# The first adjacency tiles are turned in quarters between the last rows, the loads of Y and of the sums are gated by turned rows, and the last pair's outputs are made by halves

## The chip, the cores and the metric

The kernel runs on one core of a Trainium2 chip. The metric is the device time of one execution in microseconds, the median of several runs; lower is better.

## The reference, cut to what matters

```python
scores = einsum('nd,md->nm', x @ Wq.T + bq, key @ Wk.T + bk) / sqrt(N)
s = scores * adj
s = where(abs(s) < 1e-05, -1e9, s)
u = softmax(s) @ (value @ Wv.T + bv)
x1 = layernorm(x + u @ Wm.T + bm)
out = layernorm(x1 + relu((adj @ x1) @ W1.T + b1))
```

x is 4096 x 512 in float32, adj is 4096 x 4096 of zeros and ones, every weight is 512 x 512.

## The kernel before, in words

A tile is 128 rows, so there are NT = 32 tiles of rows and columns. A float32 matrix enters TensorE as a high and a low float16 part, and a product of two such takes three passes.

The attention runs in 64 steps, g = 0 to 63: 32 tiles against the first half of the keys, then the same 32 against the second half (g = 32 + n). In a step of the second half TensorE makes the scores of tile n, the product of row tile n - 4 with W1 (`rows_product`, L895), the weighing of the values with the probabilities of tile n - 1 (`weigh`, L860) and the projection of the merged row n - 2 (`project`, L881). Between them VectorE and ScalarE mask, exponentiate, merge the two halves, normalise to x1 and split it. Every operand of TensorE that lies the wrong way round is turned by a DMA transpose which SP issues: PT from the probabilities Phl (`turn_prob`, L373 and L376), UT from the merged row Uhl (`turn_merged`, L483 and L486), x1T from the split row x1hl (`turn_x1`, L470 and L473), and AT from the adjacency matrix in bfloat16, adj_bf (`adj_tile`, L491: one tile of 128 rows by 4096 columns, 1 MB). There is one x1T and it is overwritten: the turn of row n waits until `rows_product(n - 1)` is done (y_mm).

The products of x1 with W1, called Y, go to DRAM as they come (`store_y`, L477). GpSimd loads them back in chunks of four tiles, 1 MB each (`load_y`, L698), into Y, which stays in SBUF for the last stage; chunk c has tiles 4c to 4c + 3, and the last four tiles (28 to 31) are written to Y directly. Signed sums of Y's quarters go to DRAM too, and come back as Ta and Tb (`load_sums`, L704). The places of Y, AT, Ta and Tb lie over the keys, values and probabilities, which is what some waits in SP's and GpSimd's code are for.

The last stage multiplies the adjacency matrix with Y. The rows are taken in pairs p of tiles p and 16 + p. Pairs 0 and 1 are made plainly (`aggregate(p, k, m0, m1)`, L955: matmuls for column tiles m0 to m1 of one row tile, two each), the other 14 by a scheme of seven products in place of eight (`seven`, `product`, L986), with sums of adjacency blocks (`adj_sum`, L1901) and of Y. Pair q = p - 2 has its outputs put together on VectorE (`pair`): sums of products into `csum` (L1908), sums of those (L1913), then `output` (L1856 scale and bias, L1860 relu and the row x1, L1863 statistics) and `result` (mean, nine steps of an inverse root, L1872). The four plain outputs go through the same `output` and `result`, and count on f_out. The sums of the last tiles of Y are made in between by `joined` (L1825), `last_sums` and `signed_low` (L1836).

The order of work is written out by hand, engine by engine. Each engine runs its own list in order, and waits on semaphores; SP's list is also the order in which its DMAs are issued, and all its transposes pass through it. So the tail of the attention reads on TensorE:

```python
weigh(2 * NT - 1, 1, NT - 1)
rows_product(NT - 4)
project(2 * NT - 2, 0, NT - 1)
aggregate(0, 0, 0, NP // 2)
aggregate(0, 0, NP, NP + 8)
rows_product(NT - 3)
project(2 * NT - 1, 1, NT - 1)
```

## Time and profile before

| | |
|---|---|
| median of 3 runs | 2114.94 us (2113.25 to 2116.5) |
| the profiled execution | 2114.64 us |
| its span in the trace | 2113.0 us |
| TensorE busy | 2045.3 us, 97% |
| VectorE busy | 1464.9 us, 69% |
| ScalarE busy | 675.2 us, 32% |
| granted TensorE clock, mean | 0.988 |

The times in the trace are counted from the span's start. The attention ends at about 1674 us, and the seven-product pairs begin at 1761 us. On SP and GpSimd a row of the order of time gives how long the engine was held by issuing a DMA, not how long the data took; "to landing" is the time from issue to arrival. A number in square brackets on a row is the time for which the engine stood idle before it, with what ended that.

### The profile page before, as it was taken

To read this page: it belongs to the slowest core of one execution; us is meant where nothing else is said; L and a number is where in the kernel's file an instruction comes from. 1 tells how busy PE (TensorE), PEld (TensorE's weight loads), DVE (VectorE), ACT (ScalarE), POOL (GpSimd) and SP (SyncE) were. 2 spreads that over 40 slices of the span, in tenths; PEclk is the share of its full clock that TensorE was granted. 3 is DMA by queue.
4 is the path that set the end of the run, shared out by engine and by line. 5 is a ranking of instruction groups with operands and counts; after the bars stand their busy time and mean duration, and the time that the engine had idled before them with its cause. 6 is when DMAs were issued, how large, how long until landed. Compare 5 with 4: busy or idle time off the path is not lost.

```text
span 2113.0 us, 29747 instructions
## 1 busy us (share of the span) xinstructions
PE 2045.3 (97%) x9471; PEld 980.5 (46%) x9471; DVE 1464.9 (69%) x3348; ACT 675.2 (32%) x884; POOL 81.2 (4%) x139
## 2 busy tenths in 40 slices
PE   7987999999999999999999999999999899999997
PEld 6873444444444444444444444444444334444443
DVE  3876656656565656687777777778878557877887
ACT  3343434344443434343333333333343210000000
POOL 1110000000000000000000000000000000000000
PEclk9998999999999999999999999999999999999999
DMA  7676876676667676887666666677777985554551
GB/s 244 223 271 152 189 182 151 171 162 168 160 165 176 147 172 155 216 183 161 159 163 163 163 163 163 166 170 183 186 181 211 223 239 127 131 121 119 138 133 56
DMA packets 586289, 359.56 MB, mean 170 GB/s; under 512 B 500992, under 2 KB 505088, under 8 KB 585856
## 3 DMA queue, kind: packets, MB, share of 16 engines
q1 hardware_dynamic: 564672, 275.07, 52.0%
q0 software_dynamic: 21568, 83.89, 16.4%
q8 instruction: 24, 0.39, 0.1%
q14 instruction: 25, 0.20, 0.0%
HBM read 181.15 MB, written 88.60 MB: 128 GB/s over the span
## 4 chain that ended last, share of the span: by engine, by line
PE 88%; DVE 5%; SPq 3%; DMA 3%; ACT 1%; issue 1%; DVEq 0%; ACTq 0%
PE ps L840 31%; PE ps L860 29%; PE ps L986 16%; PE ps L895 4%; PE ps L881 4%; PE ps L801 2%; SPq L491 1%; DMA stg<-in_L_gnn_value 1%; DMA wc<-in_L_gnn_Wv 1%; PE ps L785 1%; SPq L470 1%; PE ps L748 0%; DVE mcol L1378 0%; DMA x1T<-x1hl 0%; SPq L373 0%
## 5 line engine op out<-in xcount | busy, mean ns | idle before, releaser
L840 PE MATMUL ps<-KT,thl 128*128 128x512 f16 x3072 | 676.9, 380 | 9.8 <-DVE thl L1483 9.8
L860 PE MATMUL ps<-V,PT 128*128 128x512 f16 x3072 | 673.5, 379 | 0.6 <-issue 0.6
L840 PEld LDWEIGHTS ps<-KT,thl 128*128 128x128 f16 x3072 | 301.2, 98 | 375.5 <-DVE thl L1483 11.1
L860 PEld LDWEIGHTS ps<-V,PT 128*128 128x128 f16 x3072 | 300.4, 98 | 363.5 <-issue 1.9
L1510 DVE SCALAR_TENSOR_TENSOR prob<-ps,c_now,adjh 128x512 f32<-128x512 f32 x256 | 192.0, 750 | 288.9 <-PE ps L840 288.1
L1143 ACT ACTIVATE small<-prob 128x512 f32<-128x512 f32 x256 | 161.2, 630 | 630.4 <-DVE prob L1510 343.2
L1539 DVE SCALAR_TENSOR_TENSOR Phl<-prob,Phl 128x2048 f16<-128x2048 f32 x64 | 146.6, 2291 | 77.5 <-ACT Phl L1156 77.5
L1523 DVE CUSTOM_DVE_ANT_0 prob<-prob,small 128x512 f32<-128x512 f32 x256 | 174.2, 682 | 0.0
L1148 ACT ACTIVATE prob<-prob,nbias,inv 128x2048 f32<-128x2048 f32 x64 | 134.1, 2095 | 95.1 <-DVE nbias L1532 95.1
L1516 DVE TENSOR_SCALAR small<-small,eps_s,neg_s 128x512 f32<-128x512 f32 x256 | 138.9, 543 | 20.9 <-ACT small L1143 20.9
L1156 ACT ACTIVATE Phl<-prob 128x2048 f16<-128x2048 f32 x64 | 122.3, 1910 | 7.1
L1306 ACT ACTIVATE p<-ps 128x512 f32<-128x512 f32 x14 | 8.4, 597 | 333.3 <-PE ps L986 333.3
L986 PE MATMUL ps<-Y,AT 128*128 128x512 f16 x448 | 100.7, 384 | 4.5 <-DVE y L1856 4.5
L895 PE MATMUL ps<-W1T,x1T 128*128 128x512 f16 x384 | 90.7, 387 | 14.1 <-DMA x1T<-x1hl 14.1
L801 PE MATMUL ps<-xT,Aq 128*128 128x512 f32 x384 | 95.3, 398 | 1.8 <-DVE xT L1318 1.8
L681 POOL DMA_DIRECT2D adjh<-in_adj x64 | 36.2, 565 | 1387.3 <-DMA adj_bf<-adjh 782.0
L881 PE MATMUL ps<-Wvm,UT 128*128 128x512 f16 x384 | 88.2, 379 | 0.5 <-issue 0.5
L986 PE MATMUL ps<-Ta,S 128*128 128x512 f16 x336 | 79.4, 379 | 0.0
L986 PE MATMUL ps<-Tb,S 128*128 128x512 f16 x336 | 79.4, 379 | 0.0
L801 PEld LDWEIGHTS ps<-xT,Aq 128*128 128x128 f32 x384 | 69.9, 188 | 16.1 <-DVE xT L1318 2.5
L986 PEld LDWEIGHTS ps<-Y,AT 128*128 128x128 bf16 x448 | 44.2, 99 | 58.9 <-issue 7.2
L895 PEld LDWEIGHTS ps<-W1T,x1T 128*128 128x128 f16 x384 | 38.0, 99 | 61.5 <-DMA x1T<-x1hl 15.1
(177 smaller groups left out, 1737.0 us busy)
## 6 DMA issues: line engine op xcount, KB each, us to landing
adjh<-in_adj POOLq DMA_DIRECT2D x64, 512.0 KB, 5.3
adj_bf<-adjh SPq DMA_DIRECT2D x64, 512.0 KB, 4.4
t_in<-t_dram SPq DMA_DIRECT2D x64, 256.0 KB, 2.9
x_in<-in_x SPq DMA_DIRECT2D x64, 256.0 KB, 4.3
stg<-in_L_gnn_value POOLq DMA_DIRECT2D x12, 1024.0 KB, 7.4
rows<-in_x SPq DMA_DIRECT2D x32, 256.0 KB, 4.0
t_dram<-tq POOLq DMA_DIRECT2D x8, 1024.0 KB, 9.2
o_dram<-z_out SPq DMA_DIRECT2D x32, 256.0 KB, 2.7
```

The lines of the kernel that those rows point to most:

```text
L801: last = nc.tensor.matmul(ps[:, BT + e, :], Aq[:, m, k, e * P:(e + 1) * P], xT[:, b, s, k, :], start=(n == 0), stop=(n == 3 * KD - 1))
L840: last = nc.tensor.matmul(ps[:, BS + c, :], thl[:, b, s, k * P:(k + 1) * P], KT[:, m, k, c * C:(c + 1) * C], start=(n == 0), stop=(n == 3 ...
L860: last = nc.tensor.matmul(ps[:, BU + b, :], PT[:, b, s, m, :], V[:, v, m, :], start=(m == 0 and q == 0), stop=(m == MT - 1 and q == 2))
L881: last = nc.tensor.matmul(ps[:, BZ, :], UT[:, b, s, k, :], Wvm[:, m, k, :], start=(n == 0), stop=(n == 3 * KD - 1))
L895: last = nc.tensor.matmul(ps[:, BY, :].rearrange("p (o n) -> p o n", n=P), x1T[:, s, k, :], W1T[:, m, :, k, :], start=(q == 0), stop=(q == ...
L986: last = nc.tensor.matmul(ps[:, bank, :].rearrange("p (s d) -> p s d", s=2), left(m), right(m), start=(m == 0), stop=(m == NP - 1))
L1143: nc.scalar.activation(small[:, c % 2, :], prob[:, b, c * C:(c + 1) * C], ACT.Abs).then_inc(s_abs, 1)
L1148: nc.scalar.activation(prob[:, b, :], prob[:, b, :], ACT.Exp, bias=nbias[:, b:b + 1], scale=inv[:, 0:1], accum_out=rsum[:, b:b + 1]).then_ ...
L1510: nc.vector.scalar_tensor_tensor(out=prob[:, b, c * C:(c + 1) * C], in0=ps[:, BS + c, :], scalar=c_now[:, b:b + 1], in1=adjh[:, b, c * C:( ...
L1516: nc.vector.tensor_scalar(small[:, c % 2, :], small[:, c % 2, :], eps_s[:, 0:1], neg_s[:, 0:1], ALU.is_lt, ALU.mult).then_inc(s_neg, 1)
L1523: nc.vector.tensor_tensor_reduce(out=prob[:, b, c * C:(c + 1) * C], in0=prob[:, b, c * C:(c + 1) * C], in1=small[:, c % 2, :], scale=1.0, ...
L1539: nc.vector.scalar_tensor_tensor(out=Phl[:, b, LO, :], in0=prob[:, b, :], scalar=P_SCALE, in1=Phl[:, b, HI, :], op0=ALU.mult, op1=ALU.subt ...
```

## The change

Four parts.

- The turns of the first four adjacency tiles (pairs 0 and 1) are issued by quarters of 1024 columns (`adj_part`), and at other places in SP's list: the first tile and half of the second before the last probabilities are turned, the rest between turned rows. The counts that wait for AT grow by three quarters (at_in: turn + PARTS in place of turn + 1). The last load of an x tile moves ahead of the turn of merged row 62. All later adjacency tiles are turned whole, as before.
- GpSimd's loads of Y chunks 2 and 3 also wait until turned row 30 has landed, and the loads of the first two groups of sums wait for turned row 31 in place of the last projection and the last row product.
- TensorE's list between the last weighing and the plain tiles is in a new order, and the first pair's products each wait for the plain output of their own PSUM bank in place of all four. On VectorE the bias of the last x tile is added behind the last merge.
- The last pair's two outputs are made by halves of 256 columns (`last_pair`): each half's scaling, relu and statistics as soon as its sums are there.

```diff
     EARLY = 11
+
+    PARTS = 4
@@ SP
+                def adj_part(p, k, part):
+
+                    t, w = p + NP * k, N // PARTS
+                    sp.dma_start_transpose(AT[p][k][:, part * (NT // PARTS):(part + 1) * (NT // PARTS), :],
+                                           adj_bf[t * P:(t + 1) * P, part * w:(part + 1) * w]).then_inc(at_in[p][k], 16)
+
...
                         sp.wait_ge(p_lo, g)
-                        adj_tile(0, 0)
+                        for part in range(PARTS):
+                            adj_part(0, 0, part)
+
+                        sp.wait_ge(ph_in[0], 16 * NT)
+                        sp.wait_ge(pl_in[0], 16 * NT)
+                        for part in range(2):
+                            adj_part(0, 1, part)
                     turn_prob(g, b)
...
+                    if isinstance(n, int) and n == NT - 1:
+                        load_x_again(n, b)
                     if merged:
                         turn_merged(g - 1, 1 - b)
...
                 last = 2 * NT - 1
-                load_x_again(NT - 1, 1)
-
-                sp.wait_ge(ph_in[0], 16 * NT)
-                sp.wait_ge(pl_in[0], 16 * NT)
-                adj_tile(0, 1)
                 turn_x1(NT - 3)
                 store_x1(NT - 3, 1)
+                for part in range(2, PARTS):
+                    adj_part(0, 1, part)
                 turn_merged(last, 1)
+                sp.wait_ge(p_lo, 2 * NT)
+                for part in range(PARTS):
+                    adj_part(1, 0, part)
                 turn_x1(NT - 2)
                 store_x1(NT - 2, 0)
-                sp.wait_ge(p_lo, 2 * NT)
-                adj_tile(1, 0)
...
-                adj_tile(1, 1)
+                for part in range(PARTS):
+                    adj_part(1, 1, part)
@@ GpSimd
                 pool.wait_ge(ts_st, 16 * EARLY)
+
+                pool.wait_ge(x1t_in, 32 * (NT - 1))
                 for c in (2, 3):
                     load_y(c)
 
-                pool.wait_ge(z_mm, NT)
-                load_sums(0, Ta[:, 0:4, :, :, :])
+                pool.wait_ge(x1t_in, 32 * NT)
+                for c in range(2):
+                    load_sums(c, Ta[:, 4 * c:4 * c + 4, :, :, :])
                 pool.wait_ge(y_mm, NT)
-                load_sums(1, Ta[:, 4:8, :, :, :])
                 load_sums(2, Tb[:, 0:EARLY - 8, :, :, :])
@@ TensorE
                 rows_product(NT - 4)
                 project(2 * NT - 2, 0, NT - 1)
+                rows_product(NT - 3)
 
                 pe.wait_ge(s_adj, MC * 2 * NT)
-                aggregate(0, 0, 0, NP // 2)
+                aggregate(0, 0, 0, 8)
+                project(2 * NT - 1, 1, NT - 1)
                 aggregate(0, 0, NP, NP + 8)
-                rows_product(NT - 3)
-                project(2 * NT - 1, 1, NT - 1)
-                aggregate(0, 0, NP // 2, NP)
                 rows_product(NT - 2)
                 aggregate(0, 0, NP + 8, NT - TC)
-                aggregate(0, 1, 0, 12)
+                aggregate(0, 1, 0, 8)
                 rows_product(NT - 1)
-                aggregate(0, 1, 12, NT - TC)
+                aggregate(0, 1, NP, NT - TC)
+                for k in range(2):
+                    aggregate(0, k, 8, NP)
...
-                    pe.wait_ge(at_in[h][0], 16 * (turn + 1))
-                    if isinstance(q, int) and q == 0:
-                        pe.wait_ge(f_out, 2 * PLAIN)
-                    else:
+                    def plain_out(bank):
+
+                        if isinstance(q, int) and q == 0:
+                            pe.wait_ge(f_out, bank + 1)
+
+                    pe.wait_ge(at_in[h][0], 16 * (turn + PARTS))
+                    if not isinstance(q, int) or q > 0:
                         pe.wait_ge(s_cp, q)
+                    plain_out(0)
                     product(0, adj_block(h, 0, 0), upper(0))
...
@@ VectorE
                 x1_low(NT - 3, 1)
-                add_bias(1, NT - 1)
                 merge_weights(last, 1, NT - 1)
                 merge(last, 1)
                 merged_low(last, 1, NT - 1)
+                add_bias(1, NT - 1)
...
-                pair(NP - 1 - PLAIN, 1, NP // 2 - 1, None)
+                def last_pair(q):
...
+                    def half(k, side, stats, step):
+                        cols = slice(side * H, (side + 1) * H)
+                        dve.wait_ge(c_step, 11 * q + step)
+                        dve.wait_ge(out_st[k], 16 * (q + PLAIN))
+                        nc.vector.scalar_tensor_tensor(out=y[:, k, cols], in0=cs[:, k, cols], scalar=inv_y[:, 0:1],
+                                                       in1=b1_rep[:, cols], op0=ALU.mult, op1=ALU.add).then_inc(f_out, 1)
...
+                        nc.vector.scalar_tensor_tensor(out=y[:, k, cols], in0=y[:, k, cols], scalar=0.0, in1=zf[:, k, cols],
+                                                       op0=ALU.max, op1=ALU.add).then_inc(f_step, 1)
...
+                        nc.vector.bn_stats(stats[:, side, :], y[:, k, cols]).then_inc(f_step, 1)
...
+                    together(q, 1, 0, 0, 0)
+                    half(0, 0, bst, 2)
...
+                    taken(q, 7, u3[:, :], u2[:, :], ps[:, 6, :], ALU.add)
+                    half(1, 1, bst2, 6)
...
+                    together(q, 8, 0, 1, 0)
+                    half(1, 0, bst2, 9)
+                    whole(1, bst2)
...
+                    together(q, 10, 1, 0, 1)
+                    half(0, 1, bst, 11)
+                    whole(0, bst)
+
+                last_pair(NP - 1 - PLAIN)
```

TensorE, from the last weighing (V, PT) to the first of the seven products (Y, AT on the last line); W1T, x1T is a row product, Wvm, UT a projection, Y, AT a plain aggregate. Before:

```order
L860 MATMUL ps<-V,PT 128x512 x48
L895 MATMUL ps<-W1T,x1T 128x512 x12
L881 MATMUL ps<-Wvm,UT 128x512 x12
L955 MATMUL ps<-Y,AT 128x512 x32
L895 MATMUL ps<-W1T,x1T 128x512 x12
L881 MATMUL ps<-Wvm,UT 128x512 x12
L955 MATMUL ps<-Y,AT 128x512 x16
L895 MATMUL ps<-W1T,x1T 128x512 x12
L955 MATMUL ps<-Y,AT 128x512 x32
L895 MATMUL ps<-W1T,x1T 128x512 x12
L955 MATMUL ps<-Y,AT 128x512 x176
L986 MATMUL ps<-Y,AT 128x512 x32
```

and now:

```order
L877 MATMUL ps<-V,PT 128x512 x48
L912 MATMUL ps<-W1T,x1T 128x512 x12
L898 MATMUL ps<-Wvm,UT 128x512 x12
L912 MATMUL ps<-W1T,x1T 128x512 x12
L972 MATMUL ps<-Y,AT 128x512 x16
L898 MATMUL ps<-Wvm,UT 128x512 x12
L972 MATMUL ps<-Y,AT 128x512 x16
L912 MATMUL ps<-W1T,x1T 128x512 x12
L972 MATMUL ps<-Y,AT 128x512 x24
L912 MATMUL ps<-W1T,x1T 128x512 x12
L972 MATMUL ps<-Y,AT 128x512 x200
L1004 MATMUL ps<-Y,AT 128x512 x32
```

The row product of tile 29 stands directly behind the projection of row 62, and the three row products have 32 + 24 matmuls between them in place of 16 + 32; 200 plain matmuls follow the last in place of 176.

SP, from the store behind the last turned probabilities' step on (ts_dram is the sums' store, AT an adjacency turn, UT a merged row, x1T a turned row). Before, from the load of the last x tile:

```order
L351 DMA x_in<-in_x 128x512
L491 DMA_TRANSPOSE AT<-adj_bf 128x32x128
L470 DMA_TRANSPOSE x1T<-x1hl 128x4x128
L473 DMA_TRANSPOSE x1T<-x1hl 128x4x128
L461 DMA x_dram<-z_out 128x512
L483 DMA_TRANSPOSE UT<-Uhl 128x4x128
L486 DMA_TRANSPOSE UT<-Uhl 128x4x128
L470 DMA_TRANSPOSE x1T<-x1hl 128x4x128
L473 DMA_TRANSPOSE x1T<-x1hl 128x4x128
L461 DMA x_dram<-z_out 128x512
L491 DMA_TRANSPOSE AT<-adj_bf 128x32x128
L585 DMA b_rep<-in_L_gnn_b 128x512
```

and now, from the same load:

```order
L353 DMA x_in<-in_x 128x512
L485 DMA_TRANSPOSE UT<-Uhl 128x4x128
L488 DMA_TRANSPOSE UT<-Uhl 128x4x128
L512 DMA ts_dram<-Tehl 128x2048
L472 DMA_TRANSPOSE x1T<-x1hl 128x4x128
L475 DMA_TRANSPOSE x1T<-x1hl 128x4x128
L463 DMA x_dram<-z_out 128x512
L493 DMA_TRANSPOSE AT<-adj_bf 128x8x128 x2
L485 DMA_TRANSPOSE UT<-Uhl 128x4x128
L488 DMA_TRANSPOSE UT<-Uhl 128x4x128
L493 DMA_TRANSPOSE AT<-adj_bf 128x8x128 x4
L472 DMA_TRANSPOSE x1T<-x1hl 128x4x128
```

No adjacency turn stands ahead of the first turned row any more; two quarters and four stand behind it, on either side of the turn of the last merged row.

## Rows read from the trace of the kernel before

**Rows 1.** The page, busy time, share of the span and instructions of each engine.

```profile
PE 2045.3 (97%) x9471; PEld 980.5 (46%) x9471; DVE 1464.9 (69%) x3348; ACT 675.2 (32%) x884; POOL 81.2 (4%) x139
```

**Rows 2.** TensorE in order of time: start, us, what [idle before, what ended it].

```profile
1671.45 2.75 PE L881 MATMUL ps<-Wvm,UT 128*128 128x512 f16 x12 [0.46 <-issue]
1674.04 7.07 PE L955 MATMUL ps<-Y,AT 128*128 128x512 f16 x32
1692.09 5.30 PE L895 MATMUL ps<-W1T,x1T 128*128 128x512 f16 x12 [10.98 <-DMA x1T<-x1hl]
...
1716.14 2.76 PE L895 MATMUL ps<-W1T,x1T 128*128 128x512 f16 x12 [3.13 <-DMA x1T<-x1hl]
1718.74 38.15 PE L955 MATMUL ps<-Y,AT 128*128 128x512 f16 x176
1761.40 8.75 PE L986 MATMUL ps<-Y,AT 128*128 128x512 f16 x32 [4.51 <-DVE y L1856]
```

**Rows 3.** Stretch of 1692 to 1700: busy of five engines, then PEclk, DMA share, GB/s.

```profile
1692.00:1700.00 8.00, 7.91 (x25) 3.11 (x26) 1.39 (x2) 1.23 (x2) 0.00 (x0) 0.66 0.25 52
```

**Rows 4.** SP in order of time: start, us for which issuing held it.

```profile
1639.89 6.17 SPq L491 DMA_TRANSPOSE AT<-adj_bf  x1
1650.89 1.32 SPq L373 DMA_TRANSPOSE PT<-Phl  x1
...
1659.70 1.70 SPq L483 DMA_TRANSPOSE UT<-Uhl  x1
...
1665.63 14.61 SPq L491 DMA_TRANSPOSE AT<-adj_bf  x1
1680.37 7.09 SPq L470 DMA_TRANSPOSE x1T<-x1hl  x1
...
1697.48 1.19 SPq L470 DMA_TRANSPOSE x1T<-x1hl  x1
...
1715.35 5.30 SPq L491 DMA_TRANSPOSE AT<-adj_bf  x1
```

**Rows 5.** GpSimd in order of time: the loads of Y from 1658 on.

```profile
1658.07 1.49 POOL L698 DMA_DIRECT2D Y<-y_dram  x2 [63.68 <-DMA PT<-Phl]
1668.65 0.75 POOL L698 DMA_DIRECT2D Y<-y_dram  x1 [9.09 <-DMA y_dram<-Yst]
1672.83 1.49 POOL L698 DMA_DIRECT2D Y<-y_dram  x2 [3.43 <-DMA ts_dram<-Tehl]
```

**Rows 6.** Landings, 1620 to 1730: x1T, UT, AT; and Y, 1590 to 1720.

```profile
DMA to landing us min/median/max: 2.4/2.6/11.2
...
DMA to landing us min/median/max: 2.4/2.6/11.1
...
DMA to landing us min/median/max: 8.2/10.5/25.5
...
DMA to landing us min/median/max: 7.8/10.9/16.5
```

**Rows 7.** VectorE in order of time, around the last rows and outputs.

```profile
1673.24 0.69 DVE L1577 TENSOR_TENSOR x_in<-x_in,bias_o 128x512 f32<-128x512 f32 x1 [9.17 <-DMA x_in<-in_x]
...
1718.94 1.29 DVE L1825 TENSOR_TENSOR Yr<-Y 128x512 f32<-128x512 f16 x2 [11.47 <-PE ps L895]
...
1741.17 0.74 DVE L1856 SCALAR_TENSOR_TENSOR y<-ps,inv_y,b_rep 128x512 f32<-128x512 f32 x1
```

**Rows 8.** VectorE in order of time, the last pair's end.

```profile
2098.26 0.69 DVE L1908 TENSOR_TENSOR csum<-u,ps 128x512 f32<-128x512 f32 x1 [1.71 <-PE ps L986]
2098.98 0.42 DVE L1913 TENSOR_TENSOR cs<-csum 128x256 f32<-128x256 f32 x1
...
2109.96 0.55 DVE L1872 TENSOR_SCALAR y<-y,mv,rstd 128x512 f32<-128x512 f32 x1
```

**Rows 9.** GpSimd in order of time, its last store.

```profile
2088.89 0.54 POOL L709 DMA_DIRECT2D out<-y  x1 [6.67 <-DVE y L1872]
```

**Rows 10.** DMA issues of 2080 to 2113: queue, count, KB, median us to landing.

```profile
out<-y POOLq DMA_DIRECT2D x2, 256.0 KB, 2.3
```

More of the change, by code:

```diff
@@ L946, in aggregate @@
                     if m0 == 0:
-                        pe.wait_ge(at_in[p % 2][k], 16)
+                        pe.wait_ge(at_in[p % 2][k], 16 * PARTS)
                     for m in range(m0, m1):
@@ L1009, in read @@
                             pe.wait_ge(c_step, 11 * (q - 1) + step)
-                    pe.wait_ge(at_in[h][0], 16 * (turn + 1))
-                    if isinstance(q, int) and q == 0:
-                        pe.wait_ge(f_out, 2 * PLAIN)
-                    else:
+                    def plain_out(bank):
[3 more added lines that the diff above has]
+                    if not isinstance(q, int) or q > 0:
                         pe.wait_ge(s_cp, q)
+                    plain_out(0)
                     product(0, adj_block(h, 0, 0), upper(0))
                     read(1)
+                    plain_out(1)
                     product(1, adj_block(h, 0, 1), lower(0))
@@ L1024, in seven @@
                     read(4)
+                    plain_out(2)
                     product(2, adj_sum(0), signed(0))
@@ L1027, in seven @@
                     read(3)
+                    plain_out(3)
                     product(3, adj_sum(1), signed(1))
@@ L1031, in seven @@
                     product(6, adj_sum(2), signed(2))
-                    pe.wait_ge(at_in[h][1], 16 * (turn + 1))
+                    pe.wait_ge(at_in[h][1], 16 * (turn + PARTS))
                     read(8)
@@ L1895, in adj_sum @@
                         for k in range(2):
-                            dve.wait_ge(at_in[h][k], 16 * (turn + 1))
+                            dve.wait_ge(at_in[h][k], 16 * (turn + PARTS))
                     if q is not None:
@@ L1960, in _, with whole @@
                 pair(NP - 2 - PLAIN, 0, NP // 2 - 1, (1, NP // 2 - 1))
-                pair(NP - 1 - PLAIN, 1, NP // 2 - 1, None)
+                def last_pair(q):
+                    u = 2 * (q + PLAIN)
+                    done, steps = [u], [(ROOT_STEPS + 3) * u]
+                    def half(k, side, stats, step):
[4 more added lines that the diff above has]
+                                                       in1=b1_rep[:, cols], op0=ALU.mult, op1=ALU.add).then_inc(f_out, 1)
+                        done[0] += 1
+                        dve.wait_ge(zf_in[k], 16 * (q + PLAIN + 1))
+                        dve.wait_ge(f_out, done[0])
+                        nc.vector.scalar_tensor_tensor(out=y[:, k, cols], in0=y[:, k, cols], scalar=0.0, in1=zf[:, k, cols],
+                                                       op0=ALU.max, op1=ALU.add).then_inc(f_step, 1)
+                        steps[0] += 1
+                        dve.wait_ge(f_step, steps[0])
+                        nc.vector.bn_stats(stats[:, side, :], y[:, k, cols]).then_inc(f_step, 1)
+                        steps[0] += 1
+                        dve.wait_ge(f_step, steps[0])
+                    def whole(k, stats):
+                        nc.vector.bn_aggr(mv2[:, k, :], stats[:, :, :]).then_inc(f_step, 1)
+                        steps[0] += 1
+                        for step in range(ROOT_STEPS):
+                            dve.wait_ge(f_step, steps[0])
+                            inverse_root(mv2[:, k, 1:2], rv2[:, k:k + 1], ra2[:, k:k + 1], rstd2[:, k:k + 1], step).then_inc(f_step, 1)
+                            steps[0] += 1
+                        dve.wait_ge(f_step, steps[0])
+                        nc.vector.tensor_scalar(y[:, k, :], y[:, k, :], mv2[:, k, 0:1], rstd2[:, k:k + 1],
+                                                ALU.subtract, ALU.mult).then_inc(f_res, 1)
+                    dve.wait_ge(s_prod, 7 * q + 2)
+                    dve.wait_ge(s_cp, q + 1)
+                    taken(q, 1, csum[:, 0, :], p1[:, :], ps[:, 1, :], ALU.add)
+                    together(q, 1, 0, 0, 0)
+                    half(0, 0, bst, 2)
+                    dve.wait_ge(s_prod, 7 * q + 4)
+                    taken(q, 3, u2[:, :], p1[:, :], ps[:, 3, :], ALU.add)
+                    dve.wait_ge(c_step, 11 * q + 3)
+                    taken(q, 4, u5[:, :], u2[:, :], ps[:, 2, :], ALU.add)
+                    dve.wait_ge(s_prod, 7 * q + 5)
+                    dve.wait_ge(c_step, 11 * q + 4)
+                    taken(q, 5, csum[:, 1, :], u5[:, :], ps[:, 6, :], ALU.add)
+                    together(q, 5, 1, 1, 1)
+                    taken(q, 7, u3[:, :], u2[:, :], ps[:, 6, :], ALU.add)
+                    half(1, 1, bst2, 6)
+                    dve.wait_ge(s_prod, 7 * q + 6)
+                    dve.wait_ge(c_step, 11 * q + 7)
+                    taken(q, 8, csum[:, 0, :], u3[:, :], ps[:, 5, :], ALU.subtract)
+                    together(q, 8, 0, 1, 0)
+                    half(1, 0, bst2, 9)
+                    whole(1, bst2)
+                    dve.wait_ge(s_prod, 7 * q + 7)
+                    taken(q, 10, csum[:, 1, :], u5[:, :], ps[:, 4, :], ALU.add)
+                    together(q, 10, 1, 0, 1)
+                    half(0, 1, bst, 11)
+                    whole(0, bst)
```

## The prediction, made before the changed kernel was run

> **What bounds the kernel now.** I read the page first, then TensorE's order of time over the last 450 us, then the queues that feed it there, then the end. TensorE is busy for 97% of the span [rows 1], so only its gaps and the stretch after its last matmul can be won. In its order of time [rows 2] the reader is to look at the square brackets. From 1674.04 on it waits 10.98 us for a turned row, 3.13 us for the next but one, and 4.51 us for VectorE's fourth plain output: 18.6 us. It also runs slowly behind two of the three gaps: 12 matmuls take 5.30 us at 1692.09 where 12 take 2.76 us at 1716.14, and 32 take 8.75 us at 1761.40 where 32 take 7.07 us at 1674.04: 2.5 and 1.7 us more. The granted clock behind the first gap averages 0.66 of 2.4 GHz, so part of that stretch ran at 1.2 GHz [rows 3]. Behind the 3.13 us gap nothing is lost. All this is 22.8 us. Behind the last matmul comes VectorE's tail, to 2110.5 [rows 8].
>
> Why the turned row of tile 29 came late stands on SP's queue [rows 4]. A whole adjacency tile was issued at 1665.63 and held the queue for 14.61 us, and the turn of the row behind it took 7.09 us to issue, while GpSimd loaded five Y chunks of 1 MB, from 1658.07, 1668.65 and 1672.83 [rows 5]. Landings say the same [rows 6]: a turned row (x1T) lands in 2.4 us at best and 11.2 at worst, a merged one (UT) in 2.4 and 11.1, an adjacency tile in 8.2 and 25.5, a Y chunk in 7.8 and 16.5. The good values are those without big loads beside them.
>
> **The change, part by part.** I follow the new order, with the matmul price of 38.15 / 176 = 0.217 us [rows 2].
>
> *Quarters ahead of the last weights' turn.* SP now issues six quarters before the weights of tile 31 are turned, where it issued one whole tile at 1639.89 in 6.17 us. Six quarters at 6.17/4 = 1.54 us each end at 1649.1, before 1650.89 when the weights were turned [rows 4]. Cost nothing, hidden by SP's idle time up to there; without that cover each quarter delays the last weigh by its 1.5 us.
>
> *The load of the last x tile* moves ahead of the turn of merged row 62. It was issued so late that VectorE waited 9.17 us for it at 1673.24 [rows 7], with the merge and the turn of merged row 63 behind. Now the merge follows the last weigh, and the bias is added after it, hidden. But 256 KB now stand ahead of the turn of merged row 62, which landed just as TensorE needed it (0.46 us of idle at 1671.45, rows 2). No row shows that cost; it lies between nothing and 1.7 us (UT's late issue took 1.70 at 1659.70 under the Y loads; it is SP's row of this queue nearest to it, rows 4). I take 0.8, the middle, as one transfer out of several that share the engines.
>
> *Row product 29* now comes directly behind the projection of row 62, which ends at 1674.2 in the trace and at 1675.0 with the 0.8 us. Its turn waits until product 28 is done at about 1671.0; no tile is in front of it any more. At the quiet price, 1.19 us of issue for each half [rows 4] and 2.4 us to landing [rows 6], it lands at 1674.8: no wait. But Y chunk 6 is under way from 1668.65 [rows 5], and lands 7.8 us later at best, 1676.5. I take 2.0 us of waiting, for the turned row then lands near the chunk's end; bounds 0 and 7.3 (a landing of 11.2 us after 1671.1, to 1682.3).
>
> *The other quarters.* The two missing quarters of the second tile, the turn of merged row 63, four quarters of the third tile and turned row 30 follow in SP's queue: ten issues. Whole tiles in quiet take 5.30 us [rows 4], so quarters 1.3; six of them and four of 1.2 us are 12.7 us, from 1674.3 to 1687.0; with 2.4 us to landing counted from the last issue's start turned row 30 is there by 1688 to 1689. TensorE has, from 1677.0: product 29, 16 matmuls, projection 63, 16 matmuls = 56 x 0.217 = 12.2 us, to 1689.2. I take 0.3 us of waiting; bounds 0 and 3.
>
> *Row product 31.* Y chunks 2 and 3 now start only when turned row 30 has landed, about 1689, and so fall on turned row 31, issued when product 30 is done, near 1692. TensorE has 24 matmuls (5.2 us) of cover, to 1697. The two chunks land by 1697 to 1700 at 7.8 to 10.9 us [rows 6]. I take 2.5 us of waiting; bounds 0 and 6.1 with 2.5 us of slow clock, by the same late landing as above. The sums loaded behind are wanted only in the third product, 50 us on.
>
> *Outputs no longer in front of the products.* Product 0 waited for four outputs, now each product waits for its own bank. VectorE's chain starts at the end of row product 31 (1718.94), takes 22.2 us to the first output (1741.17) and ends in the fourth output, 42 us after its start [rows 2, 7]. With product 31 done at about 1702 that output comes at 1745, and the fourth product asks for it 10 us later. Cost 0: the 4.51 and 1.7 us go. Next in line is the adjacency turn for the second pair, issued when the plain tiles are done; its sums are first needed some 31 us later.
>
> *Sum for TensorE.* Its work from 1674.04 to the first product is 304 matmuls, 65.9 us. Waits: 0.8 + 2.0 + 0.3 + 2.5 = 5.6. First product: 1745.5, at full clock, where it was 1761.40 and in effect 1763.1 with the slow start. Gain 17.6 us. The fourteen rounds of seven products behind are the same.
>
> *The last pair by halves.* Half of a tile costs 0.42 us where a whole one costs 0.69, on the same operation kind [rows 8]: 0.27 us less for each of three operations in each of two outputs that stay on the tail, 1.6 us. The two halves that move forward stand in VectorE's gaps. The first waits for the store issued at 2088.89, which lands 2.3 us later [rows 9, 10] at 2091.2; with 3 x 0.5 us it ends at 2092.7, and the work up to the block sum of 2098.26 still fits, with some 0.2 us to spare. If it doesn't, up to 0.5 us is lost. Bounds 0.5 and 1.6; I take 1.6.
>
> Together 19.2 us. The profiled execution took 2114.64 us (1.64 around its span); less 19.2 that is 2095.4, and the median of the runs shown stands 0.3 above it: **2095.5 us**.
>
> *A rule against the quarters.* Rows first: with SP not held up, a half row's turn is issued every 1.2 us though each lands after 2.4 [rows 4, 6], so transfers overlap. [...]
>
> **The rivals.**
>
> *Hardly a wait is left* (0.20): Y chunk 6 does not hold up row 29 and chunks 2 and 3 do not hold up row 31. For it: TensorE's cover of 5.2 us, and less in SP's queue. Against: every turn beside Y loads was late in this trace. Waits 1.7 instead of 5.6 (0.8 and 0.9): 2091.6 us.
>
> *Each transpose lands before the next starts* (0.04). Fourteen issues of 2.6 us from 1671.0 to row product 31, and 2.9 us for stores and the last landing: it starts at 1710.3, and six quarters before the last weights' turn (15.6 us from 1639.89) delay everything by 4.6 us more, to 1714.9. It may start at 1717.1 to be even (1716.14, with 200 matmuls behind it instead of 176 and without the 6.2 us of the fourth output's wait). Gain 2.2, and 1.6 at the end: 2111 us. Against: the issue distance of 1.2 us.
>
> *Y loads starve the turned rows* (0.10): rows 29 and 31 both land as late as the worst row of the trace did, after 11.2 us. Waits 0.8 + 7.3 + 6.1, and twice the 2.5 us of slow clock: 19.3, gain 23.2 - 19.3 + 1.6 = 5.5: 2109 us. For it: two turned rows fall beside Y loads. Against: one and two chunks stand beside them, not three and a tile.
>
> *SP's queue becomes the bound* (0.04), slower: from 1671.0 on everything TensorE needs passes SP as 14 transposes in a row. At the price that the tile had under loads, 14.61/4 = 3.65 us [rows 4], row product 31 starts at 1671.0 + 51.1 + 2.9 = 1725.0, 7.9 us after the even point of 1717.1, less 1.6: 2121 us. It decides from 3.2 us a transpose on. Against: 1.2 to 1.3 us in quiet.
>
> *The waits only move* (0.02): same length at other places, 2113 us, as the tail alone.
>
> **How the numbers follow.** The forecast with waits between about 2 and 13 us has 0.60. This kernel's measurement can tell 0.2%, 4.2 us. Faster: 0.60 + 0.20 + 0.10 = 0.90. Same: the serial transposes and the moved waits, 0.06. Slower: 0.04. The range runs from the good rival less a microsecond for the runs' spread, 2090.5, to 2107, where the forecast's waits reach their bounds; outside lie the four cases of 0.10, 0.04, 0.04 and 0.02, 0.20 together.
>
> **What would show it.** TensorE's gap of 10.98 us gone, gaps of at most 3 us before row products 29 and 31, those two at 2.8 us rather than 5.3, the 4.51 us gap gone and the first products 32 in 7.07 us; the first product near 1745.5. The weigh of tile 31 still starting at 1657.9 shows that the six quarters were hidden. VectorE's add of the bias without a wait, SP's quarters at 1.2 to 1.6 us, and 1.6 us less between the last matmul and the last result. I am wrong if quarters take over 2 us to issue, if the last weigh starts later, or if a turned row lands 5 us or more after its issue with its row product waiting for it.

## The result, and the profile after

The changed kernel takes **2099.03 us** (median of 4 runs, 2098.29 to 2100.57) where the kernel before takes 2115.51 us in the runs beside it: a ratio of 0.9926 with a 95% interval of 0.9911 to 0.9941. The profiled execution took 2098.29 us, its span is 2096.6 us, 16.4 us less than before.

Here is TensorE's order of time, over the stretch of [rows 2] (start, us, what, idle before and what ended it):

```profile
1657.86 10.52 PE L877 MATMUL ps<-V,PT 128*128 128x512 f16 x48 [0.25 <-issue]
...
1671.16 2.75 PE L898 MATMUL ps<-Wvm,UT 128*128 128x512 f16 x12 [0.18 <-issue]
1675.87 4.45 PE L912 MATMUL ps<-W1T,x1T 128*128 128x512 f16 x12 [1.96 <-DMA x1T<-x1hl]
...
1689.65 2.75 PE L912 MATMUL ps<-W1T,x1T 128*128 128x512 f16 x12
1692.24 5.34 PE L972 MATMUL ps<-Y,AT 128*128 128x512 f16 x24
1700.97 4.23 PE L912 MATMUL ps<-W1T,x1T 128*128 128x512 f16 x12 [3.38 <-DMA x1T<-x1hl]
1705.03 43.33 PE L972 MATMUL ps<-Y,AT 128*128 128x512 f16 x200
1748.20 7.07 PE L1004 MATMUL ps<-Y,AT 128*128 128x512 f16 x32
```

The 10.98, 3.13 and 4.51 us gaps are gone. Left are 1.96 us ahead of row product 29 and 3.38 us ahead of row product 31. Both row products then run slowly, 4.45 and 4.23 us where the one between them takes 2.75 us: 3.2 us more together. The first seven-product pair starts at 1748.20 and at full speed, 7.07 us for 32 matmuls. The clock of these stretches, in the view of busy time by stretch (PEclk is the third number from the right):

```profile
1673.00:1680.00 7.00, 5.04 (x17) 1.82 (x15) 4.77 (x15) 0.63 (x1) 0.00 (x0) 0.76 0.99 247
1680.00:1692.00 12.00, 12.00 (x57) 5.37 (x55) 5.16 (x15) 1.23 (x2) 1.49 (x2) 1.00 0.85 167
...
1701.00:1705.00 4.00, 4.00 (x12) 1.52 (x13) 0.00 (x0) 0.00 (x0) 1.09 (x2) 0.63 0.98 210
```

It averages 0.76 and 0.63 of 2.4 GHz in the stretches of the two slow row products, so part of each ran at 1.2 GHz, and 1.00 in the stretch that follows the first.

SP's queue, as [rows 4]:

```profile
1639.96 9.05 SPq L493 DMA_TRANSPOSE AT<-adj_bf  x6
1650.97 1.97 SPq L375 DMA_TRANSPOSE PT<-Phl  x1
...
1671.06 1.20 SPq L472 DMA_TRANSPOSE x1T<-x1hl  x1
...
1674.23 2.64 SPq L493 DMA_TRANSPOSE AT<-adj_bf  x2
...
1679.55 5.45 SPq L493 DMA_TRANSPOSE AT<-adj_bf  x4
...
1695.96 11.90 SPq L493 DMA_TRANSPOSE AT<-adj_bf  x4
```

Six quarters end at 1649.0 and hide ahead of the turn of the last weights at 1650.97. The turn of row 29 starts at 1671.06 with nothing in front of it, where it started at 1680.37. The quarters cost 1.3 to 1.5 us each until 1685, and 3.0 us each from 1695.96 on, beside the loads of Y and of the sums. GpSimd's loads, as [rows 5] (the x2 is Y chunks 2 and 3), and the landings of x1T, UT, AT and Y, as [rows 6]:

```profile
1667.42 0.75 POOL L713 DMA_DIRECT2D Y<-y_dram  x1 [7.88 <-DMA y_dram<-Yst]
1689.41 1.49 POOL L713 DMA_DIRECT2D Y<-y_dram  x2 [21.24 <-issue]
1701.21 1.09 POOL L719 DMA_DIRECT2D Ta<-ts_dram  x2 [10.30 <-DMA x1T<-x1hl]
```

```profile
DMA to landing us min/median/max: 2.4/3.0/8.0
...
DMA to landing us min/median/max: 2.4/3.0/9.5
...
DMA to landing us min/median/max: 3.8/4.5/18.0
...
DMA to landing us min/median/max: 6.1/8.0/11.7
```

No turned or merged row takes 11 us to land any more, but turned row 31 and merged row 62, which stand beside Y loads, still take 8.0 and 9.5 us. The tail on VectorE, as [rows 8], with the first early half and the last result:

```profile
2076.41 0.48 DVE L1996 SCALAR_TENSOR_TENSOR y<-cs,inv_y,b_rep 128x256 f32<-128x256 f32 x1 [1.64 <-DMA out<-y]
2076.99 0.43 DVE L2001 SCALAR_TENSOR_TENSOR y<-y,zf 128x256 f32<-128x256 f32 x1
2077.46 0.43 DVE L2005 BATCH_NORM_STATS2 bst<-y 128x6 f32<-128x256 f32 x1
...
2083.43 0.69 DVE L1933 TENSOR_TENSOR csum<-u,ps 128x512 f32<-128x512 f32 x1 [0.37 <-PE ps L1004]
...
2093.60 0.55 DVE L2017 TENSOR_SCALAR y<-y,mv,rstd 128x512 f32<-128x512 f32 x1
```

A half costs 0.48, 0.43 and 0.43 us in the three operations. The early half waited 1.64 us for the store, and the block sum at 2083.43 still came on time, 0.37 us after VectorE was free.

### The profile page after: what moved, and what is told of

It reads as the page before. It is cut to its first block, busy times and chain, and to the rows that moved or that the text cites. A ratio compares the mean times of both kernels' runs of the same rounds, so it can differ in the third digit from the quotient of the medians.

```text
span 2096.6 us, 29772 instructions
## 1 busy us (share of the span) xinstructions
PE 2044.8 (98%) x9471; PEld 980.8 (47%) x9471; DVE 1466.7 (70%) x3354; ACT 676.3 (32%) x884; POOL 81.5 (4%) x139
## 3 DMA queue, kind: packets, MB, share of 16 engines
q0 software_dynamic: 21568, 83.89, 16.4%
HBM read 181.15 MB, written 88.60 MB: 129 GB/s over the span
## 4 chain that ended last, share of the span: by engine, by line
PE 93%; DVE 3%; DMA 2%; SPq 1%; ACT 1%; issue 0%; DVEq 0%; ACTq 0%
PE ps L857 31%; PE ps L877 31%; PE ps L1004 16%; PE ps L912 4%; PE ps L898 4%; PE ps L818 3%; PE ps L972 2%; DMA wc<-in_L_gnn_Wv 1%; PE ps L802 1%; DMA x1T<-x1hl 1%; PE ps L765 0%; DMA stg<-in_L_gnn_value 0%; PE ps L831 0%; DVE mcol L1403 0%; DVE tcol L1408 0%
```

## Experiments

In the labels, a_ is an edit of the changed kernel, b_ an edit of the kernel before, and f_ a further step from the changed kernel. Two stretches of every profile are compared. The first runs from the start of the last weigh (48 matmuls, V and PT) to the first product of the first pair, taken at full speed, that is, the start of its first Ta, S row less 6.91 us. The second runs from there to the end of the last result on VectorE. What comes before the last weigh is the same code everywhere, and its end varied from 1655.6 to 1663.2 us, more than most edits are worth: most of it in the first products' wait for Aq on VectorE, 5.2 to 12.5 us. The medians hold that, too. Both stretches come from one profile of each kernel, the medians and ratios from 4 to 10 runs.

| kernel | last weigh to first product | first product to last result | median, us | ratio to before, 95% interval |
|---|---|---|---|---|
| before | 105.20 | 347.43 | 2115.51 | 1 |
| changed | 90.34 | 345.95 | 2099.03 | 0.9926 (0.9911 to 0.9941) |
| changed, second time (after_again) | 91.70 | 345.95 | 2098.50 | 0.9919 (0.9904 to 0.9935) |
| a_whole | 93.46 | 345.95 | 2100.75 | 0.9918 (0.9905 to 0.9931) |
| a_nogate_y | 90.52 | 345.95 | 2098.05 | 0.9915 (0.9901 to 0.9930) |
| a_wait4 | 92.65 | 345.95 | 2100.66 | 0.9918 (0.9905 to 0.9931) |
| a_oldtail | 93.53 | 347.44 | 2100.19 | 0.9918 (0.9905 to 0.9931) |
| a_oldsums | 97.57 | 345.93 | 2105.55 | 0.9948 (0.9932 to 0.9964) |
| b_gate | 103.38 | 347.43 | 2111.65 | 0.9965 (0.9953 to 0.9976) |
| b_tile | 96.74 | 347.43 | 2108.08 | 0.9947 (0.9930 to 0.9964) |
| b_ownbank | 99.04 | 347.44 | 2109.59 | 0.9973 (0.9958 to 0.9988) |
| f_tile_behind | 92.13 | 345.94 | 2097.24 | 0.9894 (0.9877 to 0.9912) |
| f_order | 88.60 | 345.94 | 2096.55 | 0.9894 (0.9876 to 0.9911) |
| f_sums_late | 81.77 | 345.94 | 2090.98 | 0.9877 (0.9859 to 0.9896) |

The kernel before was timed again beside each group and its median was 2115.5 to 2118.3 us, so kernels of different groups are compared by ratio. The intervals reach 0.0011 to 0.0019 to either side, 2 to 4 us.

### The changed kernel again

No edit.

> The changed kernel unaltered, on the chip of these runs, as their yardstick and for its spread: the stretch from the last weigh's start to the first product was 90.3 us in its first profile and 93.5 us in the run that differed in the last pair alone. Theory one: the same gaps ahead of row products 29 and 31, of 2 to 3.5 us each, with the clock falling behind them in some runs only: 90 to 94 us. Rival: that spread came from the kernel with the old tail, and the stretch is 90.3 us again within 0.3.

91.70 us, and 93.53 us in a_oldtail, whose code is the same up to the last pair: the stretch has a spread of some 3 us of its own, by gaps that differ (2.25 us ahead of row product 30 here, none in the first profile) and by the clock. The spread is the kernel's; an effect under 3 us can't be read from one such stretch.

The gap ahead of row product 29 varies most. Seven profiles have the same loads and turns from the last weigh up to there: it is 1.95 to 1.97 us in three (after, after_again, a_wait4) and 2.60, 3.28, 4.30 and 4.57 us in a_whole, a_oldtail, a_oldsums and f_tile_behind. In the three, Y chunk 6 was issued at most 0.1 us after row product 28 began, in the four 1.0 to 2.3 us after. That the late chunk makes the gap is argued from this order; no edit tests it.

### Whole tiles instead of quarters (a_whole)

```diff
-    PARTS = 4
+    PARTS = 1
...
-                        for part in range(PARTS):
-                            adj_part(0, 0, part)
...
-                        for part in range(2):
-                            adj_part(0, 1, part)
+                        adj_tile(0, 0)
...
-                for part in range(2, PARTS):
-                    adj_part(0, 1, part)
...
+                adj_tile(0, 1)
                 turn_merged(last, 1)
                 sp.wait_ge(p_lo, 2 * NT)
-                for part in range(PARTS):
-                    adj_part(1, 0, part)
+                adj_tile(1, 0)
...
-                for part in range(PARTS):
-                    adj_part(1, 1, part)
+                adj_tile(1, 1)
```

> The changed kernel with whole adjacency tiles at the same places of SP's list (the second tile whole behind the turn of row 29, the third whole behind the turn of merged row 63). Theory one, the place in SP's list matters and not the size: a whole tile in quiet holds the queue 5.3 us where two quarters held it 2.64, so merged row 63 lands about 2.7 us later, which eats the 2.8 us that it had to spare, and the next two turned rows follow: 1 to 3 us slower than the changed kernel, about 2101 us. Rival, the size matters: the tile holds the queue 10 us or more as it did before the change, turned rows and the merged row wait behind it, 2108 us or more.

The ratio is 0.9918 where the changed kernel has 0.9919 and 0.9926, and 93.46 us lies within the spread. The whole tile behind turned row 29 held SP for 4.81 us, and merged row 63 still came in time:

```profile
1673.73 4.81 SPq L499 DMA_TRANSPOSE AT<-adj_bf  x1
```

So the rival, 2108 us or more, is refuted. The 1 to 3 us of theory one can't be told from nothing: the median, 2100.75 us, stands where it put it, the ratio doesn't. The size of the transfers is worth nothing that these runs can measure. Half of the second tile also stands at another place here, so this edit tests the cutting together with that place.

### No gate ahead of Y chunks 2 and 3 (a_nogate_y)

```diff
-                pool.wait_ge(x1t_in, 32 * (NT - 1))
                 for c in (2, 3):
                     load_y(c)
```

> The changed kernel without GpSimd's new wait ahead of Y chunks 2 and 3. Theory one: the wait only moves the loads from row 29 to row 31. Row product 29 starts some 3 us later than 1675.9 at a slow clock, merged row 63 about 1 us late, but row product 31 loses its 3.4 us gap and its slow 1.5 us: 2098 to 2103 us. Rival, the gate carries the gain: the loads beside the turn of row 29 bring back a gap of 8 us or more ahead of row product 29, 2107 us or more.

0.9915, and the same stretch, 90.52 us. TensorE's order of time shows the waits at their other places:

```profile
1678.16 4.31 PE L910 MATMUL ps<-W1T,x1T 128*128 128x512 f16 x12 [4.45 <-DMA x1T<-x1hl]
...
1693.90 2.76 PE L910 MATMUL ps<-W1T,x1T 128*128 128x512 f16 x12 [1.76 <-DMA x1T<-x1hl]
...
1702.20 2.76 PE L910 MATMUL ps<-W1T,x1T 128*128 128x512 f16 x12 [0.36 <-DMA x1T<-x1hl]
```

4.45 and 1.76 us ahead of row products 29 and 30, 0.36 us ahead of 31, where every profile with the gate and the same loads has 3.38 to 4.10. That the wait ahead of 31 is the loads' is shown by this. The 4.45 us alone shows nothing, since two profiles with the gate have about as much (4.30 and 4.57), but the two quarters behind turned row 29 now hold SP for 8.16 us instead of 2.64 to 4.98. The gate chooses which turned row meets the loads, and gains nothing in the time.

### All four outputs ahead of the first product again (a_wait4)

```diff
                         if isinstance(q, int) and q == 0:
-                            pe.wait_ge(f_out, bank + 1)
+                            pe.wait_ge(f_out, 2 * PLAIN)
```

> The changed kernel with the first product of the first pair waiting for all four plain outputs again. Theory one: the fourth output came 0.95 us after the first product's start, so a gap of about 1 us and at most 1.7 us of slow clock: 2100 to 2101.7 us. Rival, the own-bank waits are worth what the gap was before the change (4.5 + 1.7 us): 2105 us.

```profile
1676.33 2.76 PE L912 MATMUL ps<-W1T,x1T 128*128 128x512 f16 x12 [1.97 <-DMA x1T<-x1hl]
...
1750.76 7.07 PE L1004 MATMUL ps<-Y,AT 128*128 128x512 f16 x32 [0.94 <-DVE y L1881]
```

A gap of 0.94 us on the last row, with no slow start, as the 0.95 us of theory one. The ratio of 0.9918 doesn't tell it from the changed kernel's.

### The same waits in the kernel before (b_ownbank)

```diff
-                    if isinstance(q, int) and q == 0:
-                        pe.wait_ge(f_out, 2 * PLAIN)
...
+                    plain_out(0)
                     product(0, adj_block(h, 0, 0), upper(0))
                     read(1)
+                    plain_out(1)
...
+                    plain_out(2)
...
+                    plain_out(3)
```

> The kernel before, with each of the first pair's products waiting for the plain output of its own bank instead of all four. Theory one: the 4.51 us gap and the slow start of 1.7 us go, since the first product starts at once and the third finds its sums at 1757: 6.2 us less. Rival: VectorE's chain behind row product 31 holds the third or fourth product just as long, and 3 us or less is gained.

```profile
1717.53 38.15 PE L955 MATMUL ps<-Y,AT 128*128 128x512 f16 x176
1755.51 7.07 PE L986 MATMUL ps<-Y,AT 128*128 128x512 f16 x32
```

105.20 becomes 99.04: 6.2 us, and the first product follows the plain tiles at once. The same edit is worth 6.2 us in the one kernel and 0.9 us in the other. The reason is on VectorE. In the kernel before, its chain from the end of row product 31, at 1718.94, to the fourth plain output, begun at 1760.51, takes 41.6 us. There TensorE has 38.15 us of plain matmuls to cover that time. The changed kernel has 24 more behind row product 31, 43.33 us in all, and there VectorE waits for TensorE:

```profile
1748.40 0.75 DVE L1881 SCALAR_TENSOR_TENSOR y<-ps,inv_y,b_rep 128x512 f32<-128x512 f32 x1 [1.49 <-PE ps L972]
```

So either of the two, the waits by bank or the 24 matmuls, takes away nearly all of the old gap; they don't add up.

### The old tail (a_oldtail)

```diff
-                last_pair(NP - 1 - PLAIN)
+                pair(NP - 1 - PLAIN, 1, NP // 2 - 1, None)
```

> The changed kernel with the last pair's outputs made whole. Theory one: six half operations for six whole ones on the tail, 1.5 us slower, 2100.5 us, and the time from the last matmul to the last result back at 8.9 us. Rival, the halves pay nothing, since the early half waits for a store and pushes the rest: same time as the changed kernel.

347.44 us against 345.95: the halves are worth 1.49 us, and this stretch repeats within 0.02 us in all profiles. The median of 2100.19 us can't show it.

### The old waits ahead of the sums (a_oldsums)

```diff
-                pool.wait_ge(x1t_in, 32 * NT)
-                for c in range(2):
-                    load_sums(c, Ta[:, 4 * c:4 * c + 4, :, :, :])
+                pool.wait_ge(z_mm, NT)
+                load_sums(0, Ta[:, 0:4, :, :, :])
                 pool.wait_ge(y_mm, NT)
+                load_sums(1, Ta[:, 4:8, :, :, :])
```

> The changed kernel with the first group of sums loaded behind projection 63 and the second behind row product 31, as before. Theory one: 2 MB more stand beside the turn of row 31, which TensorE already waits for, so its gap grows from 3.4 us to 6 to 8 us: 2 to 5 us slower than the changed kernel. Rival: the Y chunks ahead of the sums in GpSimd's queue take the time in any case, and the gap stays: no difference.

```profile
1678.86 4.39 PE L912 MATMUL ps<-W1T,x1T 128*128 128x512 f16 x12 [4.30 <-DMA x1T<-x1hl]
...
1707.69 5.30 PE L912 MATMUL ps<-W1T,x1T 128*128 128x512 f16 x12 [7.17 <-DMA x1T<-x1hl]
```

The gap ahead of row product 31 is 7.17 us, as expected, and the ratio 0.9948, where after_again beside it has 0.9919: 0.0029, some 6 us, with intervals that just overlap. In the profile the gap and the row product behind it take 12.5 us, where five profiles with the gate have 7.6 to 9.2 us: 3.3 to 4.9 us are the gate's. The 4.30 us ahead of row product 29 lie before the edit has any effect, and are spread. So this gate is worth 3 to 6 us in the new order, more than any other edit of the changed kernel shows.

### The kernel before, Y chunks 2 and 3 gated (b_gate)

```diff
                 pool.wait_ge(ts_st, 16 * EARLY)
+                pool.wait_ge(x1t_in, 32 * (NT - 2))
```

> The kernel before, with Y chunks 2 and 3 waiting until turned row 29 has landed, and nothing else. Theory one, the tile in SP's queue was slow only because of the loads beside it: with one chunk beside it instead of three it holds the queue 7 to 9 us, turned row 29 lands by 1679, the gap of 10.98 us and its slow 2.5 us go; plain matmuls that read chunks 2 and 3 then wait 2 to 4 us: 2103 to 2107 us. Rival, the tile's place ahead of the turned row is what costs: the gap shrinks by less than 3 us, 2112 us or more.

```profile
1687.03 5.30 PE L897 MATMUL ps<-W1T,x1T 128*128 128x512 f16 x12 [5.32 <-DMA x1T<-x1hl]
1697.41 5.28 PE L883 MATMUL ps<-Wvm,UT 128*128 128x512 f16 x12 [5.07 <-issue]
```

```profile
1667.09 15.52 SPq L491 DMA_TRANSPOSE AT<-adj_bf  x1
1682.73 1.67 SPq L470 DMA_TRANSPOSE x1T<-x1hl  x1
```

My theory failed here in part, and the rival too. Without chunks 2 and 3 beside it the tile held SP for 15.52 us, no less than the 14.61 of [rows 4], so it is not these chunks that make the tile hold the queue. But it landed after 18.5 us instead of 25.5, the turn behind it took 1.67 us to issue instead of 7.09, and the gap shrank from 10.98 to 5.32 us: half of it was theirs. Then merged row 63 met the two chunks, now late. Its second half, issued at 1687.76, took 9.6 us to land, and TensorE waited 5.07 us ahead of projection 63. 1.8 us of the stretch is gained, while the ratio of 0.9965 says 5 to 10 us; with a spread of 3 us in one such stretch, the ratio is the better measure. What makes a tile in that place hold SP so long is not shown; that its data wait behind what SP issued from 1658 on, beside Y chunks 4 to 6, would fit.

### The kernel before, the tile behind turned row 29 (b_tile)

```diff
-                adj_tile(0, 1)
                 turn_x1(NT - 3)
                 store_x1(NT - 3, 1)
+                adj_tile(0, 1)
```

> The kernel before, with the second adjacency tile issued whole behind the turn and the store of row 29 instead of ahead of them, loads as before. Theory one: turned row 29 lands at 1677, ahead of need, but merged row 63 stands behind the tile and beside three loads now, lands near 1692 and leaves TensorE some 7 us idle there, with the slow clock behind it: the gap moves, 2110 to 2113 us. Rival, the place alone was the fault: both the 10.98 us and the slow 2.5 us are gained, 2102 us.

```profile
1683.13 2.75 PE L895 MATMUL ps<-W1T,x1T 128*128 128x512 f16 x12
1692.86 4.92 PE L881 MATMUL ps<-Wvm,UT 128*128 128x512 f16 x12 [6.98 <-issue]
...
1755.82 8.49 PE L986 MATMUL ps<-Y,AT 128*128 128x512 f16 x32 [4.51 <-DVE y L1856]
```

No gap ahead of row product 29, 6.98 us of waiting ahead of projection 63 and 2.2 us of slow matmuls in it, as expected. Row product 31 waits no longer either, which I had not counted, and 8.5 us are gained. With the 6.2 us of b_ownbank that makes 14.6 of the 14.9 us of the whole stretch. The two were not run together, so that they add up is argued, not shown; and 14.9 us is the first profile's, 13.5 us the second's.

### The third tile behind row 31 (f_tile_behind)

```diff
                 turn_merged(last, 1)
-                sp.wait_ge(p_lo, 2 * NT)
-                for part in range(PARTS):
-                    adj_part(1, 0, part)
                 turn_x1(NT - 2)
...
                 store_x1(NT - 1, 1)
+                sp.wait_ge(p_lo, 2 * NT)
+                for part in range(PARTS):
+                    adj_part(1, 0, part)
```

> The changed kernel with the third tile's four quarters issued behind turned row 31 instead of between merged row 63 and turned row 30. Theory one: turned row 30 lands by 1683 instead of 1688.9, so the loads of Y chunks 2 and 3 start 6 us earlier and are through by 1693, ahead of the turn of row 31; the 3.4 us gap and the slow 1.5 us go: 2094 to 2095 us. Rival: quarters and loads of sums late behind it delay the plain tiles of pair 1 or their outputs, or the loads now hold up merged row 63: 2099 us or more.

```profile
1706.12 2.76 PE L912 MATMUL ps<-W1T,x1T 128*128 128x512 f16 x12 [0.46 <-DMA x1T<-x1hl]
...
1726.09 27.80 PE L972 MATMUL ps<-Y,AT 128*128 128x512 f16 x128 [1.67 <-DMA AT<-adj_bf]
```

The gap ahead of row product 31 shrinks to 0.46 us and nothing runs slowly there. But the plain tile of pair 1 now waits 1.67 us for its adjacency turn, and in this profile row product 29 waited 4.57 us, so the stretch is no shorter. The ratio is 0.9894, with an interval that overlaps the changed kernel's. Theory one held for the gap; the new wait is one that the rival had named. The median of 2097.24 us lies between the two forecasts.

### A new order on TensorE (f_order)

On top of f_tile_behind:

```diff
-                rows_product(NT - 3)
                 aggregate(0, 0, 0, 8)
-                project(2 * NT - 1, 1, NT - 1)
+                rows_product(NT - 3)
                 aggregate(0, 0, NP, NP + 8)
+                project(2 * NT - 1, 1, NT - 1)
                 rows_product(NT - 2)
                 aggregate(0, 0, NP + 8, NT - TC)
                 aggregate(0, 1, 0, 8)
+                aggregate(0, 1, NP, NP + 8)
                 rows_product(NT - 1)
-                aggregate(0, 1, NP, NT - TC)
+                aggregate(0, 1, NP + 8, NT - TC)
```

> The same, and on TensorE 16 plain matmuls moved ahead of row product 29, 16 between it and projection 63, none between projection 63 and row product 30, and 40 before row product 31. Theory one: the 2.0 us gap with its slow 1.7 us goes too, no gap is left from 1671 to the products, which begin at 1740: 2090 to 2092 us. Rival: x1 of row 31 or merged row 63 becomes the late one, or VectorE's outputs hold the products: 2094 us or more.

```profile
1674.90 2.75 PE L912 MATMUL ps<-W1T,x1T 128*128 128x512 f16 x12
...
1694.76 2.75 PE L912 MATMUL ps<-W1T,x1T 128*128 128x512 f16 x12
...
1713.66 30.70 PE L972 MATMUL ps<-Y,AT 128*128 128x512 f16 x128 [4.06 <-DMA AT<-adj_bf]
```

```profile
1692.70 24.04 SPq L493 DMA_TRANSPOSE AT<-adj_bf  x8
```

No row product waits. One wait has taken the place of all: 4.06 us for the adjacency turn of pair 1, with the slow clock behind it (30.70 us for 128 matmuls that take 27.80). Eight quarters took 24.04 us beside the loads of the sums. Neither side of the expectation had named it. The median of 2096.55 us misses the 2090 to 2092 of theory one, and the ratio is that of f_tile_behind, 0.9894: the order by itself shows no gain.

### The sums behind the third tile (f_sums_late)

On top of f_order:

```diff
                 pool.wait_ge(x1t_in, 32 * NT)
+                pool.wait_ge(at_in[1][0], 16 * PARTS)
```

> The kernel with the third tile behind row 31 and the new TensorE order, and GpSimd's loads of the first sums wait for the third tile as well. Theory one: in the run before the only wait left was the plain tile of pair 1 for that adjacency turn, 4.06 us and 2.9 us of slow clock behind it, because eight quarters stood beside 5.5 MB of sums for 24 us; with the loads behind the third tile it lands by 1702 and both go. From the last weigh's start to the first product 81 to 82 us, where the changed kernel takes 90 to 94: some 9 us less than the changed kernel on the same chip. Rival: the sums, the fourth tile or the second pair's adjacency now come late for the first pair: 85 us or more in that stretch, or a gap within the first pair.

```profile
1682.78 2.75 PE L913 MATMUL ps<-W1T,x1T 128*128 128x512 f16 x12
...
1702.64 2.75 PE L913 MATMUL ps<-W1T,x1T 128*128 128x512 f16 x12
1705.23 39.88 PE L973 MATMUL ps<-Y,AT 128*128 128x512 f16 x184
1744.94 7.07 PE L1006 MATMUL ps<-Y,AT 128*128 128x512 f16 x32
```

```profile
1700.65 11.96 SPq L493 DMA_TRANSPOSE AT<-adj_bf  x8
```

Nothing is left to wait for: 81.77 us, all 304 matmuls at 0.217 us behind projection 62. The same eight quarters hold SP for 11.96 us now, half of the 24.04. The ratio is 0.9877 (0.9859 to 0.9896), 2090.98 us against 2098.50 us of the changed kernel on the same chip. This version beats both kernels, by 25 and 7.5 us.

## Why the prediction was right

Forecast 2095.5 us, measured 2099.03: the direction, the likeliest mechanism and its places were right, 16.4 us of the 19.2 us came. (The forecast's last step has a slip: 2095.4 and 0.3 make 2095.7.)

- *Quarters ahead of the last weights' turn*, cost nothing: right. They end at 1649.0 (forecast 1649.1), and the last weigh starts at 1657.86 as before.
- *The load of the last x tile*, 0.8 us: projection 62 waited 0.18 us, less than before. Other profiles show 0.1 to 1.1 us. VectorE's add of the bias had no wait.
- *Row product 29*, 2.0 us: 1.96 us, but 1.95 to 4.57 us in the six other profiles with the same loads and turns up to there. *Row product 30*, 0.3: none in this profile, 0 to 2.25 us in the others. *Row product 31*, 2.5: 3.38 us, and 3.38 to 4.10 in the profiles with the same loads.
- The waits together: 5.5 us, forecast 5.6. That they agree so well is partly luck: four other profiles with the same loads (after_again, a_whole, a_wait4, a_oldtail) have 7.3 to 8.2 us. The places and the order of size are what was foreseen. **The term that failed** is the clock: I put no slow matmuls behind these gaps, by one row where 3.13 us of idle had cost nothing. They cost 1.7 and 1.5 us. The first product is 2.7 us late (1748.20 against 1745.5), for the other terms gave 0.5 us back.
- Two of the forecast's own signs of being wrong came. Turned row 31 landed 8.0 us after its issue with its row product waiting, and the last four quarters took 3.0 us each to issue. The first cost 3.38 us and the slow matmuls behind it, the second nothing, as these quarters stand behind row 31. The two row products also ran at 4.45 and 4.23 us where 2.8 had been foreseen.
- *Outputs no longer in front of the products*: the result is right, the fourth output came at 1749.15 us and held nothing, but the cause is given to the wrong edit. The 6.2 us are the waits' by bank in the kernel before (b_ownbank); in the changed kernel the old wait would have cost 0.9 us only (a_wait4), because of the 24 matmuls moved behind row product 31. The forecast's own numbers say so: an output at 1745 and a first product at 1745.5 leave nothing to wait for.
- *The halves*, 1.6 us: 1.49. The reserve of 0.2 us was 0.37.
- Read wrongly as a cause: I took the tile's 14.61 us in the queue for the loads' doing. b_gate shows that the two later loads are not behind it, though half of the 10.98 us gap goes with them, and b_tile that without the tile in front of the turned row the whole gap goes. The sum didn't rest on this, since the change takes away both.
- Quarters without big loads beside them were issued every 1.3 to 1.5 us and landed 3.8 to 5.2 us after their issue, so they overlap, and whole tiles in their place gave the same time within the noise. Of the rivals, the serial transposes and SP's queue as the bound are refuted by these rows, hardly a wait by the 5.5 us, and the moved waits by the 16.4 us. Loads beside turned rows were real, at less than half of the price that this rival had: 5.3 us of waiting and 3.2 us of slow matmuls against 13.4 and 5.0 us.
- The Trainium skill (DMA: Bandwidth & Descriptors, "Anatomy of one DMA") gives a DMA on GpSimd's path a fixed part of about 2.0 us beside the time for its bytes. The turns here are issued by SP, and no such part shows as time between them in its queue. No run here measures it on GpSimd's path.

## What to carry to other kernels

In a hand-written order with one queue for all transposes, ask for every transfer who waits for what stands behind it: moving one tile behind a turned row, alone, was worth more than half of the whole gain, while cutting it into quarters gave nothing that could be measured. A gate on a load pays only if the load then runs where nobody is about to wait; otherwise it moves the gap. When the last gap of a stretch is closed, look at once for the transfer that the new order made late, for here it took three more edits until all the waits were gone. And when two edits of one change can each close the same gap, don't count it for one of them before it has been taken out alone.

## What the runs showed of the hardware that was not expected

The clock behind a short gap is not told by the gap's length. Row product 29 ran in 4.45 us behind 1.96 us of idle in the first profile of the changed kernel, and in 2.76 us behind 1.95 us in the second:

```profile
1674.49 2.76 PE L912 MATMUL ps<-W1T,x1T 128*128 128x512 f16 x12 [1.95 <-DMA x1T<-x1hl]
...
1689.01 2.76 PE L912 MATMUL ps<-W1T,x1T 128*128 128x512 f16 x12 [2.25 <-DMA x1T<-x1hl]
```

Before the change 3.13 us of idle had cost nothing [rows 2], and in b_ownbank 3.93 us at nearly the same place made the row product take 4.31 us. In a_oldtail and a_whole gaps of 3.5 and 3.9 us were followed by a row product of 5.30 us. In f_order 4.06 us were followed by 2.9 us of slow matmuls. Behind gaps of 5 us and more the matmuls were slow in every profile, by 1.5 to 2.5 us in the row product or projection right behind. So in these profiles a gap of 2 to 4 us carries a price of 0 to 2.9 us that none of the edits controls, and that is a part of the stretch's spread.

The second surprise is how a whole queue slows: a quarter takes 1.3 to 1.5 us to issue in quiet, and 3.0 us where loads of sums run beside it. The same eight quarters held SP for 24.04 us beside these loads in f_order, and for 11.96 us in f_sums_late, where the loads came later.
